# A conditioned layer norm and MLP on one core: another order for the first batch, and a last batch by token tiles

## The reference, cut to what matters

```python
def _ln(x, g, b):
    m = jnp.mean(x, axis=-1, keepdims=True)
    v = jnp.mean((x - m) ** 2, axis=-1, keepdims=True)
    return (x - m) * jax.lax.rsqrt(v + EPS) * g + b

def _mlp_ln(s, W1, b1, W2, b2, g, b):
    h = jax.nn.silu(s @ W1 + b1) @ W2 + b2
    return _ln(h, g, b)

h = _ln(_ln(x, pw_g[pathway_ids], pw_b[pathway_ids]), cp_g[compartment_ids], cp_b[compartment_ids])
t = _ln(x, tm_g[time_steps], tm_b[time_steps])
m = x + _mlp_ln(memory_state, mem_...)[:, None, :]      # n and r alike, with noise and resource
s = _ln(x, ms_g[scale_type], ms_b[scale_type])
w = jax.nn.softmax(aw)
cat = jnp.concatenate([w[0]*h, w[1]*t, w[2]*m, w[3]*n, w[4]*r, w[5]*s], axis=-1)
out = x + _mlp_ln(cat, int_W1, int_b1, int_W2, int_b2, int_g, int_be)
```

## Time and profile before

| | |
|---|---|
| median of 3 runs | 1005.12 us |
| the profiled execution's own time | 1006.83 us |
| its span in the trace | 1005.1 us |
| TensorE matmuls busy | 971.1 us, 97% |
| VectorE busy | 806.9 us, 80% |
| GpSimd busy | 516.3 us, 51% |
| ScalarE busy | 267.9 us, 27% |
| DMA | 141.66 MB, mean 141 GB/s |

### The profile page before, as it was taken

One profiled execution on the slowest core, in us unless ns is written; L12 is line 12 of the kernel. 1 busy time (PEld: TensorE's weight loads), 2 busy tenths in 40 slices (PEclk: granted clock), 3 DMA queues, 4 the chain that ended last, 5 costly groups with the idle time before them and its releaser, 6 DMA issues.

```text
span 1005.1 us, 13647 instructions
## 1 busy us (share of the span) xinstructions
PE 971.1 (97%) x4408; PEld 798.8 (79%) x4408; DVE 806.9 (80%) x1110; ACT 267.9 (27%) x330; POOL 516.3 (51%) x620
## 2 busy tenths in 40 slices
PE   3999999999999999999999999999999999999994
PEld 2866788888888888888888888888888888888883
DVE  7798879798787978878698887869888796978845
ACT  3522323231332222133122313222231322223120
POOL 4453447465553746455374645637454563744311
PEclk9899999999999999999999999999999999999998
DMA  9764545535354462535445363544536365443121
GB/s 338 239 238 138 167 117 160 154 90 182 89 177 121 157 154 79 195 84 180 123 157 139 90 199 77 184 126 156 135 85 198 84 188 126 156 134 76 44 62 42
DMA packets 52593, 141.66 MB, mean 141 GB/s; under 512 B 10184, under 2 KB 10440, under 8 KB 48480
## 3 DMA queue, kind: packets, MB, share of 16 engines
q0 software_dynamic: 22976, 66.07, 26.2%
q1 hardware_dynamic: 29600, 75.37, 21.6%
HBM read 124.52 MB, written 16.90 MB: 141 GB/s over the span
## 4 chain that ended last, share of the span: by engine, by line
PE 94%; DVE 4%; DMA 1%; issue 1%; SPq 0%; ACT 0%; POOL 0%; DVEq 0%; POOLq 0%
PE hid_ps L1198 23%; PE hid_ps L1200 23%; PE hid_ps L1199 23%; PE o_ps L1287 5%; PE o_ps L1288 5%; PE o_ps L1289 5%; PE made_ps L1178 3%; PE made_ps L1191 3%; PE hid_ps L1203 1%; DMA keep<-int_W 1%; DVE cat_lo L729 0%; PE o_ps L1118 0%; PE o_ps L1155 0%; DVE w_raw L895 0%; DVE fst L832 0%
## 5 line engine op out<-in xcount | busy, mean ns | idle before, releaser
L1198 PE MATMUL hid_ps<-cat_hi,w_hi 128*128 128x512 f32 x1024 | 403.6, 394 | 2.0 <-POOL w_lo L485 1.0
L1200 PE MATMUL hid_ps<-cat_hi,w_lo 128*128 128x512 f32 x1024 | 400.3, 391 | 0.0
L1199 PE MATMUL hid_ps<-cat_lo,w_hi 128*128 128x512 f32 x1024 | 400.3, 391 | 0.0
L1198 PEld LDWEIGHTS hid_ps<-cat_hi,w_hi 128*128 128x128 f32 x1024 | 193.4, 189 | 43.0 <-DVE cat_lo L790 1.4
L1200 PEld LDWEIGHTS hid_ps<-cat_hi,w_lo 128*128 128x128 f32 x1024 | 193.2, 189 | 40.8
L1199 PEld LDWEIGHTS hid_ps<-cat_lo,w_hi 128*128 128x128 f32 x1024 | 193.4, 189 | 39.3
L467 POOL DMA_INDIRECT pw_rows<-cp,class_now x64 | 128.6, 2010 | 73.7 <-DVE y_sb L798 63.4
L610 ACT ACTIVATE cat_hi<-v_ring 128x1024 fp32r<-128x1024 f32 x64 | 68.0, 1062 | 304.5 <-DVE v_ring L780 304.5
L460 POOL DMA_INDIRECT pw_rows<-pw,path_now x64 | 96.8, 1513 | 62.2 <-DVE y_sb L816 41.3
L415 POOL TENSOR_TENSOR fve<-fmv,eps_col 128x1 f32<-128x1 f32 x64 | 38.9, 608 | 155.9 <-DVE fmv L835 155.9
L481 POOL DMA_DIRECT2D r_sb<-x x60 | 58.0, 966 | 108.2 <-DVE r_sb L864 97.6
(11 more groups left out here) (137 smaller groups left out, 1203.5 us busy)
## 6 DMA issues: line engine op xcount, KB each, us to landing
x_sb<-x SPq DMA_DIRECT2D x16, 1024.0 KB, 6.2
xc<-xT SPq DMA_DIRECT2D x16, 1024.0 KB, 5.1
out<-r_sb SPq DMA_DIRECT2D x64, 256.0 KB, 2.0
r_sb<-x POOLq DMA_DIRECT2D x60, 256.0 KB, 4.7
stats_bc<-token_stats SPq DMA_DIRECT2D x30, 256.0 KB, 5.1
ids_sb<-ids SPq DMA_DIRECT2D x16, 256.0 KB, 7.3
keep<-int_W SPq DMA_DIRECT2D x12, 256.0 KB, 6.6
w_raw<-int_W SPq DMA_DIRECT2D x12, 256.0 KB, 9.4
```

Source lines behind the costliest of these rows:

```text
L1198: pe.matmul(acc, w1_hi[:, k, cols], hi, start=start, stop=False)
L1199: pe.matmul(acc, w1_hi[:, k, cols], lo, start=False, stop=False)
L1200: return pe.matmul(acc, w1_lo[:, k, cols], hi, start=False, stop=stop)
```

## The change

- **The loads** of the first batch come in another order: half of `xT`, one group of three `keep` blocks, x, the tables, the next group, the other half of `xT`, ids, two groups, two blocks of `int_W1`, the networks' tiles, four blocks, the row ids, six blocks. The first of three blocks of a group has a semaphore of its own.
- **TensorE** begins with `warm(18)`: 18 products of a 128x128 tile of ones with itself. `x_high_part(k)` needs only the high part of block k of the weights, `x_low_part(k)` the low part. Between them stand `warm(4)`, the mean (`mean_first`) and deviations (`dev_first`).
- **Engines.** The mean's and the rest's diagonals are made by ScalarE, `sum_low` and the class table's low part by VectorE, the split of the reciprocal root by GpSimd; `batch_copy` and half of `class_rows` go to ScalarE. `onehots(0)` is cut in two.
- **The small networks.** `nets_hidden` takes the conditions as weights (32 columns) and streams the network's weights, 512 columns, into 32 rows for each network; `nets_rows` copies them and four transposes turn them.
- **Batch 1** has an order of its own: on TensorE each `pair` comes before the next `fill`, `second(0, t)` one pair later; on VectorE `w2_low` and part of y move behind the first `ts_mult`; x(2)'s statistics follow later.
- **The last batch.** All `last_pairs` run first, then the second layer tile by tile. `b2` comes as a product of ones with a row and its rounding rest, so `last_stats` reads PSUM without an addition before it. `last_sum` is put in another order.
- `sT` grows from 16 to 32 columns for each of four chunks.

```diff
+            pool.memset(sel_all, 1.0).then_inc(sel_ready, 1)     # first of the memsets
...
             sp.dma_start(small_sb[:, :], small).then_inc(small_in, 16)
+            load_xT_half(0)
+            keep_load(0)
             load_x(0)
-            load_xT(0)
...
+            keep_load(1)
+            load_xT_half(1)
+            load_ids(0)
+            keep_load(2)
+            keep_load(3)
+            mod_load(FT)
+            mod_load(FT + 1)
             for n in NET:
                 stage_load(n)
+            for i in range(FT + 2, FT + 6):
+                mod_load(i)
+            sp.dma_start(row_ids[:, :], pid).then_inc(row_ids_in, 16)
...
@@ GpSimd, chunk
-                if first:
-                    x_rstd(b + 1)
-                    net_rstd()
                 if not last:
                     path_ids(b + 1)
                     gather(b + 1, 0)
                     gather(b + 1, 1)
+                if first:
+                    net_rstd()
+                    x_rstd(b + 1)
@@ GpSimd, behind the last chunk
+            pool.wait_ge(filled, 6 * (BATCHES - 1) + FT)
+            pool.wait_ge(used, 6 * (BATCHES - 1) + 1)
+            pool.memset(scaled[:, :].bitcast(f32), 0.0).then_inc(b2_cleared, 1)
+            pool.memset(onehot[:, 0:P].bitcast(f32), 1.0).then_inc(b2_cleared, 1)
+            pool.wait_ge(b2_cleared, 2)
+            for at in (0, 32):
+                pool.tensor_copy(scaled[at:at + 1, :], b2_bc[at:at + 1, :]).then_inc(b2_rounded, 1)
+            pool.wait_ge(b2_rounded, 2)
+            pool.tensor_tensor(scaled[32:33, :], b2_bc[32:33, :], scaled[32:33, :].bitcast(f32),
+                               ALU.subtract).then_inc(b2_ready, 1)
@@ ScalarE, opening
+            x_high(0, 0)
             act.wait_ge(mix_ready, 1)
-            x_high(0, 0)
             sum_first(0)
-            x_high(0, 1)
+            sum_high(0)
             act.wait_ge(table_in, 16 * 6)
             act.activation(class_tab[:, :, :], tab_raw, ACT.Copy).then_inc(tab_hi_done, 1)
-            sum_high(0)
             sum_first(1)
+            x_high(0, 1)
+            sum_high(1)
             sum_first(2)
-            sum_high(1)
+            mean_diagonal()
+            sum_high(2)
             sum_first(3)
-            sum_high(2)
+            rest_diagonal()
             sum_high(3)
@@ VectorE, first chunk, opening (as it is after)
+                class_columns()
+                x_low(0, 0)
+                sum_blocks(0)
+                x_stats(0, 0)
+                sum_low(0)
+                x_stats(0, 1)
+                x_stats(0, 2)
+                x_stats(0, 3)
+                sum_blocks(1)
+                tab_low()
+                sum_low(1)
+                x_low(0, 1)
+                sum_blocks(2)
+                dev_diagonal()
+                sum_low(2)
+                sum_blocks(3)
+                scaled_first()
+                sum_low(3)
+                centre_tile(0)
+                ts_mult(0, 0)
+                w_low(4)
+                w_low(5)
+                centre_tile(1)
+                ts_low(0, 0)
+                ts_mult(0, 1)
@@ VectorE, first chunk, end (as it is after)
+                y_norm (four), w_low(13), nets_stats, h_low(0, 0), w_low(14), w_low(15), x_stats(1, 0),
+                h_low(0, 1), nets_norm, class_rows, x_stats(1, 1..3), x_low(1, 0), nets_weigh, x_low(1, 1),
+                onehot_next(1), y_mul(1, 0), y_mul(1, 1), add_b1, centre(1), scaled_next(1), y_add(1, 0)
@@ VectorE, last batch
-            for t in range(TT):
-                out_stats(BATCHES - 1, t, last_ps[t])
-                if t > 0:
-                    last_sum(t - 1)
-            last_sum(TT - 1)
+            last_stats(0)
+            last_stats(1)
+            last_sum(0)
+            last_stats(2)
+            last_sum(1)
+            last_sum(2)
+            last_stats(3)
+            last_sum(3)
@@ TensorE
+            def nets_hidden():
+                for c in range(NETS + 1):
+                    n, depth = max(c - 1, 0), tiles[NET[c]][1]
+                    stage_wait(pe, NET[c])
+                    pe.matmul(o_ps[32 * n:32 * n + 32, 0, :], sT[0:depth, c, :], stage[NET[c] % STAGE][0:depth, :],
+                              start=(c != 1), stop=(c != 0)).then_inc(pe_used, 1)
+            def last_second(t):
+                if t >= 2:
+                    pe.wait_ge(o_done, TT * (BATCHES - 1) + t - 3)
+                cols = slice(t * P, (t + 1) * P)
+                if t == 0:
+                    pe.wait_ge(b2_ready, 1)
+                pe.matmul(last_ps[t], onehot[:, 0:P], scaled[:, :], start=True, stop=False)
+                for k in range(FT):
+                    if t == 0:
+                        pe.wait_ge(last_lo_done, k + 1)
+                    pe.matmul(last_ps[t], hid_hi[:, k, cols], w2_hi[:, k, :], start=False, stop=False)
                     pe.matmul(last_ps[t], hid_lo[:, k, cols], w2_hi[:, k, :], start=False, stop=False)
                     ins = pe.matmul(last_ps[t], hid_hi[:, k, cols], w2_lo[:, k, :], start=False, stop=(k == FT - 1))
+                ins.then_inc(second_done, 1)
             def first_chunk():
-                spread_first()
-                x_pairs()
-                for n in range(NETS):
-                    nets_hidden(n)
+                pe.wait_ge(sel_ready, 1)
+                warm(WARM[0])                  # 18
+                x_high_part(0)
+                x_low_part(0)
+                warm(WARM[1])                  # 4
+                x_high_part(1)
+                x_low_part(1)
+                mean_first()
+                x_high_part(2)
+                x_low_part(2)
+                dev_first()
+                x_high_part(3)
+                fill(0, 0)
+                x_low_part(3)
+                nets_hidden()
                 fill(0, 1)
                 pair(0, 2)
+                nets_hidden_turn()
...
             def chunk(b, last=False):
                 if isinstance(b, int) and b == 1:
                     first_pair(b)
                     fill(b, 0)
+                    pair(b, 1)
+                    fill(b, 1)
+                    pair(b, 2)
+                    fill(b, 2)
+                    second(b - 1, 0)
+                    pair(b, 3)
+                    fill(b, 3)
+                    second(b - 1, 1)
+                    pair(b, 4)
+                    second(b - 1, 2)
```

More of the change, by code:

```diff
@@ L160, in build @@
         sum_in = [sem(f"sum_in{k}") for k in range(FT)]
+        sum_more_in = [sem(f"sum_more_in{k}") for k in range(FT)]
         stage_in = [sem(f"stage_in{i}") for i in range(STAGE)]
@@ L1038, in first_chunk @@
-                for k in range(FT):
-                    w2_low(k)
+                centre(1)
+                scaled_next(1)
                 y_add(1, 0)
-                y_add(1, 1)
-                y_norm(1, 0)
-                y_norm(1, 1)
-                dve.wait_ge(rows_bc_in, 16)
             def chunk(b, last=False):
-                ts_mult(b, 0)
-                hidden_low(b - 1, 0)
-                ts_low(b, 0)
-                hidden_low(b - 1, 1)
-                y_mul(b, 2)
-                y_mul(b, 3)
@@ L1063, in chunk @@
                     x_stats(b + 1, 0)
                     x_stats(b + 1, 1)
-                ts_mult(b, 3)
-                out_sum(b - 1, 0)
-                ts_low(b, 3)
-                out_stats(b - 1, 1, o_ps[:, 1, :])
-                if not last:
+                    out_stats(b - 1, 1, o_ps[:, 1, :])
+                    out_sum(b - 1, 0)
                     x_stats(b + 1, 2)
+                    h_low(b, 0)
                     x_stats(b + 1, 3)
-                out_sum(b - 1, 1)
-                out_stats(b - 1, 2, o_ps[:, 0, :])
@@ L1074, in chunk @@
-                h_low(b, 0)
-                out_sum(b - 1, 2)
-                if not last:
-                    x_low(b + 1, 0)
-                h_low(b, 1)
+                    out_stats(b - 1, 2, o_ps[:, 0, :])
+                    h_low(b, 1)
+                    out_sum(b - 1, 1)
+                    x_low(b + 1, 0)
+                    out_sum(b - 1, 2)
+                else:
+                    ts_mult(b, 0)
+                    hidden_low(b - 1, 0)
+                    ts_low(b, 0)
+                    hidden_low(b - 1, 1)
+                    y_mul(b, 2)
+                    y_mul(b, 3)
+                    ts_mult(b, 1)
+                    y_add(b, 2)
+                    ts_low(b, 1)
+                    y_add(b, 3)
+                    y_norm(b, 2)
+                    ts_mult(b, 2)
+                    y_norm(b, 3)
+                    ts_low(b, 2)
+                    out_stats(b - 1, 0, o_ps[:, 0, :])
+                    if not last:
+                        x_stats(b + 1, 0)
+                        x_stats(b + 1, 1)
+                    ts_mult(b, 3)
+                    out_sum(b - 1, 0)
+                    ts_low(b, 3)
```

(11 more changed lines are left out.)

381 lines of the change are left out of this document (206 added, 175 removed).

## The result

The kernel after runs in 994.64 us (median of 4 runs, 992.23 to 994.98) against 1005.1 us for the kernel before in the same comparison: ratio 0.9886, 95% interval 0.9874 to 0.9898. The forecast was 988.0 us with a range of 983.5 to 994.5, so the median lies 0.14 us past the range's upper end. The profiled execution took 994.5 us, with a span of 992.8 us. Between the two profiled executions lie 12.3 us, between the medians 10.5; 17.1 were forecast.

What follows compares the result with a forecast made beforehand. TensorE was busy 971.1 of 1005.1 us, so gains lay before batch 2 and behind the last matmul. First batch 10.5, batch 1 1.5, batch 2 -1.2, tail 6.3: 17.1 us less, 988.0 us; range 983.5 to 994.5.

Steps and rivals of the forecast that it cites:

- opening of x: From the start to the networks' layer: new load order and VectorE's chain bring TensorE there at 27.6, 5.2 us less.
- networks' layer and turning: Small networks' first layer: 4.2 us becomes 2.2 (bounds 1.2 to 3.7) plus 0.35 for four transposes, 1.65 us less.
- clock behind it: Behind the thin networks' layer, 36.99 to about 42.9: matmuls no longer 0.43 us apart, 2.8 us less.
- stall at `pair(0, 2)`: First batch: TensorE, ready at 30.2, waits for VectorE's `ts_low(0, 0)` until 31.3; 1.1 us more, between 0 and 3.
- `h_low` waits: First batch: TensorE's two waits for `h_low`, at 74.30 and 77.77, go; 2.0 us less.
- batch 1: `pair(1, 1)` between the fills covers TensorE's wait for batch 1's first `ts_mult`; 1.5 us less.
- batch 2: `out_sum(0, 2)` waits for GpSimd's root, so batch 2's first `ts_mult` is about 1.5 us late; 1.2 us more (0 to 3).
- last batch: Tail by token tiles: three tiles finish before the last matmul, so the last sum starts at 993.95; 6.3 us less.
- the rival priced at 993: VectorE's opening chain ends at 29 in place of 26, losing 3 + 1 + 1 us; 25%.
- the clock rival: Opening: TensorE's idle stretches let the clock fall back to 1.2 GHz, giving 990 to 991 us; 10%.
- the slower rival: VectorE enters the loop late and doesn't catch up, 1.5 us in each of 13 batches: 1007 to 1008 us; 3%.
- The contention that the prediction feared: Last batch: VectorE and GpSimd contend for SBUF, `b2`'s row comes nearer 980 and the tail gains 5.5 us.

Runs made afterwards that it cites:

- rows_later: Kernel after, with the load of the three rows (`rows_bc`, 768 KB) held until scaled(1) is made; 993.63 us, ratio 0.9892.
- gathers_later: Kernel after, with GpSimd holding four gathers of batch 1 until that batch's spread statistics have landed; 992.31 us, ratio 0.9869.
- warm_none: Kernel after without the products on ones, at the start and between the blocks; 993.25 us, ratio 0.9881.
- nets_order: Kernel after, with the four products of the networks' first layer issued in the order 0, 2, 3, 1; 993.67 us, ratio 0.9881.
- nets_full: Kernel after, with the networks' four first-layer products all 128 rows deep and in the order 0, 2, 3, 1; 993.13 us, ratio 0.9877.
- tail_only: Kernel before with the last batch of the kernel after and nothing else; 998.64 us, ratio 0.9942.
- nets_thin: Kernel after with the networks' first layer of the kernel before (16 columns streamed, result not turned); 994.21 us, ratio 0.9894.
- both_mended: Kernel after with batch 2's last x statistics ahead of the low parts and four batch 1 gathers held for the spread statistics; 989.45 us, ratio 0.9842.
- stats2_early: Kernel after, on VectorE only: x_stats(2, 3) moved ahead of h_low(1, 0) and out_sum(0, 1) behind it; 992.58 us, ratio 0.9874.

## Why the prediction was right in direction and too large

| step | forecast, us less | in the profiled executions | verdict |
|---|---|---|---|
| opening of x | 5.2 | 4.2 | right, 1.0 too large |
| networks' layer and turning | 1.65 | 0.15, all of it and more from the clock | wrong |
| clock behind it | 2.8 | 2.8 | as read, but a chance and not a term |
| stall at `pair(0, 2)` | -1.1 | 0 | did not come, see below |
| `h_low` waits | 2.0 | 2.0 | right |
| batch 1 | 1.5 | 0.2 | wrong |
| batch 2 | -1.2 | -3.9 | mechanism right, price three times as high |
| last batch | 6.3 | 6.8 | right |
| sum | 17.1 | 12.3 | |

The median moved by less, 10.5 us. The forecast of 988.0 took the 1.7 us by which the profiled execution of before lies above its median over to the kernel after; there the two agree (994.5 and 994.64). That makes 1.8 of the 6.6 us between forecast and median, and the table the other 4.8. That the median comes out at the edge of the range at all is luck: the upper end was set for a longer VectorE chain, which did not come, and the losses at the networks, batch 1 and batch 2 filled that room instead.

*The opening.* The first product of x starts at 10.62 (forecast 9.75 to 10.2) and TensorE reaches the networks at 28.55 (27.6). x landed about 1 us later than my 2.9 us per MB had it (statistics at 11.07 against 10.1), and VectorE's chain, the rival priced at 993, ended with `scaled_first` at 26.3 (25.58 + 0.75) where I had 25.8 to 26. So VectorE's operations did not stretch: the sums took 1.54 again, `x_low(0, 1)` 1.22 and not the 3.39 of the earlier trace rows. The clock did fall behind the first idle stretch, as the clock rival had it. It cost nothing there that can be told: rows_later had 1.00 throughout the opening, longer waits instead (6.4 us against 4.5), and its networks' layer at 28.73. Where it fell later (gathers_later, warm_none) the layer came 1.4 to 1.8 us later.

*The networks.* This is the step that failed by its reasoning. I took 2.2 us, with the three column groups beside each other as in the earlier trace rows. The products contract 128, 128, 64 and 32 rows, and each took 0.94 us alone, 3.77 in all, which was my upper bound "all in series". nets_order showed that the shared group isn't the reason, nets_full that the heights are: 1.84 us with equal ones. The Trainium skill ("TensorEngine Tiling (Array Packing)", Key Properties) says that changing the tiling mode drains the engine while tiles of one mode run in parallel. These rows agree with both halves. I had cited it and then counted the drain as included in a row in which all tiles had one mode. I should have looked at whether the mode changes here. The term was too large from its other side as well: of the 4.2 us of the thin layer 0.43 were the slow clock (tail_only: 3.77). At one clock the new form gains nothing and pays 0.28 for its transposes. That the layer took so long also hid the forecast stall at `pair(0, 2)`: in nets_full TensorE is 1.9 us earlier and it stands there, 0.97 us. Net, the two steps together were to give 0.55, and gave 0.15.

*The clock behind the thin layer.* The earlier trace rows show it for one execution. tail_only, with the same thin layer, had no drop; nets_thin had one, of 3.4 us. Counted with the 0.43 inside the layer it cost 3.2 us in the kernel before. I took 2.8 us, read in one execution, off a median of several. A part of the difference between 12.3 (profiles) and 10.5 (medians) may be this; no trace of a second execution of before shows it.

*Batch 1.* The wait between the two fills did go, as forecast. A new one took its place: `centre(1)` was to come at 80 to 82 and came at 86.76, since the statistics took 6.2 us to land; the kernel before needed 3.7. I had written "covered by 1 to 3 us", from an order in which the first gather was issued at 74.78, 2.4 us after the statistics. In the new order four gathers are issued at 77.82 to 82.42, around that transfer:

```profile
77.82 1.05 POOL L483 DMA_INDIRECT pw_rows<-pw,path_now  x1 [0.53 <-issue]
78.90 1.10 SPq L347 DMA_DIRECT2D stats_bc<-token_stats  x2
...
82.42 0.95 POOL L490 DMA_INDIRECT pw_rows<-cp,class_now  x1 [0.30 <-issue]
```

gathers_later shows that they are the cause: landing 4.0, batch 1 59.39 us, and 61.04 - 59.39 = 1.65, which is close to the 1.5 forecast. The gain was there and was spent on a transfer. The chain ahead of it was late too: the transfer was issued at 78.90, and with a fast landing `centre(1)` still came at 84.41 (both_mended), later than the 80 to 82, but in time.

*Batch 2.* The chain was the one written down: the root for `out_sum(0, 2)` behind batch 2's statistics on GpSimd, then `ts_mult` late. But the lateness was 2.5 us and not 1.5 (7.3 against 4.8 us into the batch), so the stall was 2.03 us. Then the clock stood at 0.50 to 0.60 for the next 4 us, with 0.43 us between matmuls, for another 1.9. I had priced a stall at its length. stats2_early takes it away whole. Once in the loop, VectorE caught up, as forecast: no waits in batches 3 to 14, so the slower rival fell.

*The last batch.* The last sum starts 2.44 us after the last matmul, 2.9 forecast. GpSimd's row of `b2` was ready in time; it ended at 972.26 and its first use is at 973.59. The contention that the prediction feared was there, without a price: beside GpSimd's two copies (968.87, 1.71 us) VectorE's two low parts took 2.11 us (1.42 in the kernel before), and GpSimd's subtraction took 1.60, more than the 0.7 to 1.3 of the forecast.

The two waits that were not foreseen in their size, 1.5 us at batch 1 and 3.9 at batch 2, are what both_mended recovers. Its 989.45 us lies between 985.5 and 990.5, where the forecast saw the kernel after, but it is another kernel and no point for the forecast.

## What to carry to other kernels

When a change saves time ahead of a joint between engines, list what each queue issues in the new order during the transfers at that joint. A transfer time read in the kernel before holds only for its neighbours of then.

Price a stall of TensorE at its length, and as a bad case at its length plus 2 us. Take a slow stretch that one execution shows as a chance, not as a term.

Products on column groups overlapped here only between neighbours of one height. Pad the short ones with zeros where the rows are free, and then look for what the earlier end will wait for next.

## What the runs showed of the hardware

- **A stall costs twice, sometimes.** At the joints of batches 1 and 2, over all traces of the new opening, nine waits of TensorE of 0.97 to 1.85 us cost their length and 0.2 to 0.3 more (length of the batch against 59.39 or 58.93 without a wait). Seven waits of 1.90 to 2.23 us went two ways: five cost 3.8 to 4.1 us, with the granted clock at 0.5 (that is 1.2 GHz) for 3 to 4 us behind them; two (rows_later at batch 2, warm_none at batch 1) cost 2.1 to 2.5 with the clock held; what decides between the two ways stays open. The Trainium skill ("TensorE: Matmul & The Clock Gate", What's actually happening) has throttled as the default and activity as what releases it; the stretches behind idle time agree.
- **The clock is not the same in two executions of one opening.** gathers_later and rows_later differ from the kernel after only behind their opening, and yet the slow stretch of the opening lay at 10.6 to 13.6 in the kernel after, at 16.8 to 23.8 in gathers_later and nowhere in rows_later. In warm_none the first product of x at 11.56 ran four matmuls in 2.04 us, the slow pace (1.20 at the fast one), while the granted clock of that stretch reads 1.00. The kernel before is the same: matmuls 0.43 apart from 18.21 to 22.05, granted clock 1.00. So in the opening the pace of the matmuls is the reading to trust.
- **Small transfers beside gathers take 1.5 to 2 times as long.** Two transfers of statistics, 256 KB each, landed in 4.0 to 4.1 us without gathers and in 6.2 to 8.5 us beside four gathers of 1.57 MB on another queue.
